# Squares of adj turned in place through three places, most mask pieces made by GpSimd, and a transposed copy with longer runs, in a four-layer graph network

## The chip, the cores and the metric

The kernel runs on one core of a Trainium2 chip. The metric is the time of one execution on the device in microseconds; less is better. The profile is one execution of the same program, taken by the hardware profiler. Its span is counted from the first to the last instruction, and the profiled execution's own time is a little more than its span. Engines are named as TensorE (PE), VectorE (DVE), ScalarE (ACT), GpSimd (POOL) and SyncE (SP), which here does nothing but issue DMAs and wait.

## The reference

There are 4096 nodes with 256 features in `x`, and a dense float32 `adj` of 4096 x 4096 in which about one entry in 130 isn't zero. Every layer is followed by a residual and a LayerNorm.

```python
def layer0(x, adj):                       # 4 heads of 64
    q, k, v = split(x @ Wqkv + bqkv)      # per head
    scores = q @ k.T * 64 ** -0.5 + graph_bias * adj
    scores = where(adj == 0, -1e9, scores)
    return softmax(scores) @ v @ Wout + bout
def layer1(x, adj):
    Wh = x @ W
    e = leaky_relu((Wh @ a[:256])[:, None] + (Wh @ a[256:])[None, :], 0.2)
    return softmax(where((adj > 0) | eye, e, -9e15), axis=1) @ Wh
def layer2(x, adj):                       # d = adj.sum(axis=1) ** -0.5
    return (d[:, None] * adj * d[None, :]) @ x @ W.T + b
def layer3(x, adj):
    return relu((d[:, None] * adj * d[None, :]) @ x @ W)
for layer in (layer0, layer1, layer2, layer3):
    x = layernorm(x + layer(x, adj))
```

## The kernel before, in words

The whole program is written by hand: every engine has its own list of instructions, in an order that the code fixes, and semaphores tie the lists together. There is no scheduler.

**Layer 0** (`layer0_attention`, to about 1740 us of the span) takes the 4096 rows in 16 chunks of 256. A chunk is a loop of 32 *beats*, numbered `at` = 8h + j for four heads h and eight pieces j of 128 x 1024 scores. In each beat TensorE makes one piece of scores (four matmuls, line 513) for the beat 12 later and VectorE reads it (line 757: it adds the bias, writes to a ring of probabilities and keeps the row maximum). TensorE has one PSUM place for such a piece, so the read must be over before TensorE's next scores. Besides, TensorE transposes earlier probabilities (line 525) in one beat and aggregates with the values (line 538) in odd beats, projects a finished head (line 547) at j = 3, and makes queries at the end of odd heads. ScalarE takes exponentials (643) and copies transposed probabilities out of PSUM (652).

The *bias* of a chunk (graph_bias * adj, plus a huge negative number where adj is zero) has eight pieces of 128 x 1024. While a chunk runs, the bias of the next is made in place: piece i is loaded by SyncE at beat 12 + i (`load_bias`, 341); VectorE makes a mask of it (`mask_bias`, 715: is_equal, to bf16) and then the bias (`make_bias`, 723). `BIAS_PARTS` says how many of these sixteen steps stand in which beat, 14 to 26. There is one buffer for masks. From beat 20 on, reads of scores use the new bias.

Layer 0 also writes `adjT`, a copy of adj in DRAM in which squares of 32 x 32 are transposed, for layers 2 and 3. It is made in 256 *blocks* of 128 x 512: SyncE loads a block (`load_block`, 352), VectorE turns it (`turn_block`, 777), SyncE stores it with four DMAs (`store_block`, 362). Before, a chunk has 16 blocks, in its odd beats; the last chunk has its 16 in two beats of three up to beat 23. A block is turned from one of two input buffers into one of two output buffers. SyncE stores block b in the beat after its turn, then loads block b + 2, and then, in even beats, waits until TensorE has aggregated in the next odd beat and reloads that quarter of the values (`load_values`, 337); next stand x and bias loads. All this is one queue, in this order. GpSimd has a power for each chunk's LayerNorm and the store of the chunk's rows.

The last chunk makes no bias. In its beats VectorE and SyncE do early work for layer 1 instead (`early_sync`: loads of x and of adj rows, of 2 MB each).

**Layer 1** (`graph_layers`, about 1740 to 2370 us) works on 8 chunks of 512 rows; masks of adj > 0 are made on VectorE and on GpSimd (line 1040), and `degrees` (1206) computes d, as 128 x 32 numbers, on GpSimd.

**Layers 2 and 3** (to the end) are 16 runs of 512 rows. Each run reads adjT in *sets* of 512 keys, four DMAs of 256 KB per set (`load_set`, 1126), with the four 32-row groups of a tile in separate pieces of 2 KB. The rows of x that meet them are loaded by `load_row_tile` (1142), scaled by d and split into a high and a low part (`split_hi`, 1454 on ScalarE, `split_lo` on VectorE). TensorE multiplies three times for each pair of tiles (1374 to 1376).

Of the kernel before, what the change touches and what calls it, by code (L numbers as in the profile page):

```python
# [23 lines left out]
P = 128  # L24
N = 4096
# [112 lines left out]
class Shared:  # L138


    def __init__(self, space, x1_stored):
# [3 lines left out]
        self.block_stored = [space.sem(f"block_stored{k}") for k in range(2)]  # L145
# [3 lines left out]
def layer0_attention(nc, shared, x, adj, Wqkv, bqkv, Wout, bout, graph_bias, v_heads, value_stored, x1, x1_stored, adjT):  # L149

# [23 lines left out]
    BIAS_PARTS = {14: 1, 15: 1, 16: 2, 17: 1, 18: 1, 19: 1, 20: 2, 21: 1, 22: 1, 23: 1, 24: 2, 25: 1, 26: 1}  # L174
# [14 lines left out]
    CHUNK_BLOCKS = CT * BLOCK_SETS  # L189
    BLOCKS = CHUNK_BLOCKS * CHUNKS  # L190
    SQUARE = 32
    SQUARES = P // SQUARE
    BLOCK_BEATS = tuple(range(1, CHUNK_BEATS, 2))
    LAST_BLOCK_BEATS = (1, 2, 4, 5, 7, 8, 10, 11, 13, 14, 16, 17, 19, 20, 22, 23)
    x_tiles, adj_tiles, x1_tiles, w_rows = tiles_of(x), tiles_of(adj), tiles_of(x1), tiles_of(Wqkv)
    with ExitStack() as ctx:
        sp = Space(nc, ctx, "at")
        kT = sp.sb("kT", [P, H, N], F32R)
        probs = sp.sb("probs", [P, 2 * CT * N])
        bias = sp.sb("bias", [P, CT, N])  # L200
        q = sp.sb("q", [P, 3, 2, CN], F32R)
        masked = sp.sb("masked", [P, PIECE], BF16)
# [19 lines left out]
        first = probs[:, 0:CT * N]  # L222
        ring = probs[:, 2 * CT * N - PLACES * CT * PIECE:].rearrange("p (k t n) -> p k t n", k=PLACES, t=CT)
        squares = probs[:, 0:4 * BLOCK].rearrange("p (a b n) -> p a b n", a=2, b=2)
# [15 lines left out]
        bk = first[:, 7680:7682]  # L240
# [20 lines left out]
        block_loaded = [sp.sem(f"block_loaded{k}") for k in range(2)]  # L261
        block_turned = sp.sem("block_turned")
        block_stored = shared.block_stored
        masked_ready = sp.sem("masked_ready")
# [19 lines left out]
        shared.blocks_stored = 16 * SQUARES * BLOCKS // 2  # L284
# [20 lines left out]
        def block_in(c, at):  # L305

            beats_of = LAST_BLOCK_BEATS if c == CHUNKS - 1 else BLOCK_BEATS
            return CHUNK_BLOCKS * c + beats_of.index(at) if at in beats_of else None

        def block_at(b):  # L310

            return b // CHUNK_BLOCKS * CT + b % CT, b % CHUNK_BLOCKS // CT

# [20 lines left out]
        def sync_program(sync, early):  # L334
# [15 lines left out]
            def load_block(b):  # L350
                row_tile, n = block_at(b)
                sync.dma_start(squares[:, 0, b % 2, :], adj_tiles[:, row_tile, n * BLOCK:(n + 1) * BLOCK])\
                    .then_inc(block_loaded[b % 2], 16)

            def store_block(b):
# [4 lines left out]
                for g in range(SQUARES):  # L360
                    at = row_tile % BLOCK_TILES * P + g * SQUARE
                    sync.dma_start(to[:, row_tile // BLOCK_TILES * BLOCK_SETS + n, :, at:at + SQUARE],  # L362
                                   squares[g * SQUARE:(g + 1) * SQUARE, 1, b % 2, :]
                                   .rearrange("j (k i) -> j k i", i=SQUARE))\
                        .then_inc(block_stored[b % 2], 16)
# [65 lines left out]
        def gpsimd_program(pool):  # L431
# [15 lines left out]
            for c in range(CHUNKS):  # L447
                finish(c)
# [1397 lines left out]
```

## Time and profile before

| what | before |
| --- | --- |
| time, median of 3 runs | 3175.77 us (3172.98 to 3178.01) |
| profiled execution, its own time | 3172.68 us |
| its span | 3170.9 us |
| TensorE busy | 3017.0 us, 95% |
| VectorE busy | 2140.6 us, 68% |
| ScalarE busy | 1893.5 us, 60% |
| GpSimd busy | 364.5 us, 11% |
| hardware DMA queue, share of 16 engines | 72.9% |
| granted clock of TensorE, mean | 0.99 |

A busy share is an average over four layers with different limits. What a change in one of them is worth is read from that stage: from the reads of scores for layer 0, since each stands for one beat, and from the chain of waits at the joints between layers.

### The profile page before, as it was taken

The numbers are of one execution on the slowest core, as the hardware profiler recorded it, in microseconds if no ns is written. First come the engines' busy times: TensorE is split into PE (matmuls) and PEld (weight loads), VectorE is DVE, ScalarE is ACT, GpSimd is POOL, SyncE is SP. The second block draws the span as 40 slices with busy tenths as digits, with TensorE's granted clock in tenths as the row PEclk, the third lists the DMA queues.
The fourth block names the chain that finished last, engine by engine and source line by source line (L and its number), as shares of the span: only waits on it lengthen the run. The fifth ranks groups of instructions, "written<-read, shape, count | busy, mean of one in ns | idle before, by whom it ended". The sixth has DMA issues, their size and how long they took to land.

```text
span 3170.9 us, 45180 instructions
## 1 busy us (share of the span) xinstructions
PE 3017.0 (95%) x16612; PEld 2174.3 (69%) x16612; DVE 2140.6 (68%) x3588; ACT 1893.5 (60%) x2705; POOL 364.5 (11%) x196
## 2 busy tenths in 40 slices
PE   8899999999999999999996899999999999799998
PEld 6676677766776677767774555555558888678886
DVE  6677776777677776777675787777635545464554
ACT  3677767676777677776764577776663333343342
POOL 2000000000000000000000355554500000000000
PEclk9999999999999999999998999999999999899999
DMA  6688888888888888888899433333169989699982
GB/s 184 129 166 175 182 170 158 171 180 180 157 168 176 181 176 155 172 178 182 164 158 241 154 113 146 127 143 129 47 163 220 210 201 205 158 207 209 205 196 58
DMA packets 768588, 530.48 MB, mean 167 GB/s; under 512 B 563568, under 2 KB 599408, under 8 KB 768368
## 3 DMA queue, kind: packets, MB, share of 16 engines
q1 hardware_dynamic: 762096, 506.61, 72.9%
q0 software_dynamic: 6272, 20.98, 2.0%
q8 instruction: 133, 2.18, 0.3%
q14 instruction: 87, 0.71, 0.1%
HBM read 439.36 MB, written 88.08 MB: 166 GB/s over the span
## 4 chain that ended last, share of the span: by engine, by line
PE 77%; DVE 8%; DMA 7%; issue 4%; SPq 2%; ACT 2%; DVEq 0%; POOL 0%; POOLq 0%; ACTq 0%
PE at_score L513 13%; PE gl_four L1324 12%; PE at_o L538 12%; PE at_turn L525 10%; PE gl_quad L1374 7%; PE gl_quad L1375 7%; PE gl_quad L1376 7%; PE gl_quad L1307 3%; DMA at_bias<-in_adj 3%; PE at_mixed L547 2%; DMA gl_early<-x 2%; DVE at_probs L757 2%; PE gl_four L1349 2%; DVE at_bias L723 2%; SPq L362 1%
## 5 line engine op out<-in xcount | busy, mean ns | idle before, releaser
L757 DVE CUSTOM_DVE_ANT_0 at_probs<-at_score,at_bias 128x1024 f32<-128x1024 f32 x509 | 621.1, 1220 | 338.5 <-PE at_score L513 335.8
L652 ACT ACTIVATE at_pT<-at_turn 128x1024 f32<-128x1024 f32 x512 | 521.2, 1019 | 333.7 <-PE at_turn L525 332.3
L513 PE MATMUL at_score<-at_kT,at_q 128*128 128x512 f32 x2036 | 610.8, 422 | 69.2 <-DVE at_maxima L757 68.8
L643 ACT ACTIVATE at_probs<-at_probs,at_minus_max 128x1024 f32<-128x1024 f32 x512 | 585.8, 1144 | 39.3 <-DVE at_minus_max L762 38.3
L538 PE MATMUL at_o<-at_pT,at_values 128*64 128x256 f32 x4096 | 502.0, 387 | 22.4 <-DMA at_values<-v_heads 22.4
L525 PE MATMUL at_turn<-all_ident,at_probs 128*128 128x128 f32 x4096 | 489.8, 273 | 0.0
L525 PEld LDWEIGHTS at_turn<-all_ident,at_probs 128*128 128x128 f32 x4096 | 463.4, 140 | 35.6 <-issue 1.7
L513 PEld LDWEIGHTS at_score<-at_kT,at_q 128*128 128x128 f32 x2036 | 350.7, 189 | 196.5 <-DVE at_maxima L757 127.7
L1324 PE MATMUL gl_four<-gl_early,gl_first_wh 128*128 128x512 f32 x1024 | 460.7, 593 | 1.9 <-ACT gl_early L1442 1.9
L1467 ACT ACTIVATE gl_split<-gl_units 128x1024 fp32r<-128x1024 f32 x256 | 263.6, 1055 | 276.8 <-PE gl_quad L1376 276.8
L538 PEld LDWEIGHTS at_o<-at_pT,at_values 128*64 128x64 f32 x4096 | 272.2, 137 | 227.7 <-issue 93.9
L1374 PE MATMUL gl_quad<-gl_split,gl_rows_hi 128*128 128x512 f32 x1024 | 406.1, 397 | 21.8 <-DVE gl_split L1655 21.8
L1375 PE MATMUL gl_quad<-gl_split,gl_rows_hi 128*128 128x512 f32 x1024 | 401.6, 392 | 0.0
L1376 PE MATMUL gl_quad<-gl_split,gl_rows_lo 128*128 128x512 f32 x1024 | 401.3, 392 | 0.0
L1655 DVE TENSOR_TENSOR gl_split<-gl_units,gl_split 128x1024 fp32r<-128x1024 f32 x256 | 306.1, 1221 | 115.9 <-ACT gl_split L1467 115.5
L1324 PEld LDWEIGHTS gl_four<-gl_early,gl_first_wh 128*128 128x128 f32 x1024 | 184.7, 190 | 186.4 <-issue 184.1
L1040 POOL TENSOR_SCALAR gl_first_weights<-gl_first_weights 128x1024 f32<-128x1024 f32 x57 | 238.3, 4181 | 275.3 <-ACT gl_first_weights L1424 275.3
L1374 PEld LDWEIGHTS gl_quad<-gl_split,gl_rows_hi 128*128 128x128 f32 x1024 | 194.2, 190 | 65.3 <-DVE gl_split L1655 24.9
L1442 ACT ACTIVATE gl_early<-gl_quad 128x1024 f32<-128x1024 f32 x128 | 130.9, 1022 | 159.6 <-PE gl_quad L1307 159.6
L1376 PEld LDWEIGHTS gl_quad<-gl_split,gl_rows_lo 128*128 128x128 f32 x1024 | 194.1, 190 | 40.9
L1375 PEld LDWEIGHTS gl_quad<-gl_split,gl_rows_hi 128*128 128x128 f32 x1024 | 194.3, 190 | 40.3 <-issue 0.2
L777 DVE STREAM_TRANSPOSE at_probs<-at_probs 128x512 f32<-128x512 f32 x256 | 180.9, 707 | 27.6 <-DMA at_probs<-in_adj 26.5
(121 smaller groups left out, 2650.4 us busy)
## 6 DMA issues: line engine op xcount, KB each, us to landing
gl_units<-adjT SPq DMA_DIRECT2D x512, 256.0 KB, 7.7
at_bias<-in_adj SPq DMA_DIRECT2D x128, 512.0 KB, 6.9
at_values<-v_heads SPq DMA_DIRECT2D x256, 256.0 KB, 4.0
at_probs<-in_adj SPq DMA_DIRECT2D x256, 256.0 KB, 5.0
adjT<-at_probs SPq DMA_DIRECT2D x1024, 64.0 KB, 4.0
gl_first_weights<-in_adj SPq DMA_DIRECT2D x32, 2048.0 KB, 8.1
gl_early<-x SPq DMA_DIRECT2D x24, 512.0 KB, 4.6
x<-gl_early POOLq DMA_DIRECT2D x16, 512.0 KB, 3.9
```

What stands on the lines that cost most here:

```text
L513: last = pe.matmul(place[:, at], q[:, q_place(h), part, t * P:(t + 1) * P], kT[:, h, col:col + BANK], start=part == 0, stop=part == 1)
L525: last = pe.transpose(turn_bank[j % 2][:, a * CN + t * P:a * CN + (t + 1) * P], ring[:, place_in_ring(s, m // BEATS), t, m % BEATS * P:(m ...
L538: last = pe.matmul(o_bank[side * HD:(side + 1) * HD, 0:CN], values[:, q, a, :], pT[:, slot, a % GROUP * CN:(a % GROUP + 1) * CN], start=q ...
L643: act.activation(part, part, ACT.Exp, bias=minus_max[:, k, t:t + 1], scale=1.0, accum_out=sums[:, k, t, pp:pp + 1]).then_inc(prob_ready, 1)
L652: act.activation(pT[:, j % PT_SLOTS, :], turn_bank[j % 2][:], ACT.Copy).then_inc(pT_ready, 1)
L757: dve.tensor_tensor_reduce(out=ring[:, place_in_ring(u, pp), t, :], in0=place[:], in1=bias[:, t, at], scale=SCALE, scalar=LOWEST, op0=ALU. ...
L1324: last = pe.matmul(out_bank1[c % 2][half], wh[:, m * D + half * P:m * D + (half + 1) * P], pT[:, g % PT_RING, part * CN:(part + 1) * CN], ...
L1374: pe.matmul(out_bank3[r % 2][half], rows_hi[:, at], block_hi, start=first, stop=False)
L1375: pe.matmul(out_bank3[r % 2][half], rows_hi[:, at], block_lo, start=False, stop=False)
L1376: last = pe.matmul(out_bank3[r % 2][half], rows_lo[:, at], block_hi, start=False, stop=final)
L1467: act.activation(split3[:, slot, 0, :], tiles[:, n, part:part + 2 * CN], ACT.Copy).then_inc(hi3_ready, 1)
L1655: dve.tensor_tensor(split3[:, slot, 1, :], tiles[:, n, part:part + 2 * CN], split3[:, slot, 0, :].bitcast(F32), ALU.subtract).then_inc(lo3 ...
```

## The change

Three things change in layer 0 and one in what layers 2 and 3 read.

1. The blocks are turned in place, in three buffers in place of two pairs. SyncE waits, before it loads block b + 2, until block b - 1 has been stored from the same place. The 256 blocks now stand in 17 beats of each chunk, `BLOCK_BEATS`, most of them even; 15 chunks take 255 blocks and the last chunk one.
2. Six of the eight mask pieces of a chunk's bias are made by GpSimd, as soon as the load has landed and the bias of two pieces before is made; there are two buffers for masks. VectorE makes the last two, in beats 24 and 25. The makes stand in beats 17, 18, 20, 21 and 23 to 26. On GpSimd the finish of a chunk now comes before the masks of the same turn of the loop.
3. The load of a set is one DMA of 1 MB with runs of four rows, 8 KB. The keys of a set so arrive in another order; `load_row_tile` loads the rows of x in the same order, and GpSimd makes a permuted copy of d in 32 small copies (`row_scale`), for which the first `split_hi` waits.
4. The views of a few layer 0 buffers move, and `masked` gets two places.

```diff
-        self.block_stored = [space.sem(f"block_stored{k}") for k in range(2)]
+        self.block_stored = [space.sem(f"block_stored{k}") for k in range(3)]
...
-    BIAS_PARTS = {14: 1, 15: 1, 16: 2, 17: 1, 18: 1, 19: 1, 20: 2, 21: 1, 22: 1, 23: 1, 24: 2, 25: 1, 26: 1}
+    MAKE_BIAS = {17: 0, 18: 1, 20: 2, 21: 3, 23: 4, 24: 5, 25: 6, 26: 7}
+    MASK_BIAS = {24: 6, 25: 7}
+    POOL_MASKS = 6
...
-    BLOCK_BEATS = tuple(range(1, CHUNK_BEATS, 2))
-    LAST_BLOCK_BEATS = (1, 2, 4, 5, 7, 8, 10, 11, 13, 14, 16, 17, 19, 20, 22, 23)
+    BLOCK_BEATS = (0, 2, 4, 6, 8, 10, 12, 13, 15, 18, 19, 21, 22, 26, 27, 29, 30)
...
-        probs = sp.sb("probs", [P, 2 * CT * N])
+        masked = sp.sb("masked", [P, 2, PIECE], BF16)
+        probs = sp.sb("probs", [P, BLOCK_PLACES * BLOCK + PLACES * CT * PIECE])
...
         def block_in(c, at):
 
-            beats_of = LAST_BLOCK_BEATS if c == CHUNKS - 1 else BLOCK_BEATS
-            return CHUNK_BLOCKS * c + beats_of.index(at) if at in beats_of else None
+            b = len(BLOCK_BEATS) * c + BLOCK_BEATS.index(at) if at in BLOCK_BEATS else BLOCKS
+            return b if b < BLOCKS else None
...
             def load_block(b):
                 row_tile, n = block_at(b)
-                sync.dma_start(squares[:, 0, b % 2, :], adj_tiles[:, row_tile, n * BLOCK:(n + 1) * BLOCK])\
-                    .then_inc(block_loaded[b % 2], 16)
+                sync.dma_start(squares[:, b % BLOCK_PLACES, :], adj_tiles[:, row_tile, n * BLOCK:(n + 1) * BLOCK])\
+                    .then_inc(block_loaded[b % BLOCK_PLACES], 16)
...
                         if b + 2 < BLOCKS:
+                            wait(sync, block_stored[(b + 2) % BLOCK_PLACES], 16 * SQUARES * ((b + 2) // BLOCK_PLACES))
                             load_block(b + 2)
...
+            def mask_bias(c, i):
+
+                t, pp = piece_at(i)
+                pool.wait_ge(adj_loaded[i], 16 * (c + 1))
+                pool.wait_ge(bias_ready, BEATS * c + i - 1)
+                pool.tensor_scalar(masked[:, i % 2, :], bias[:, t, pp * PIECE:(pp + 1) * PIECE], 0.0, MASKED / SCALE,
+                                   ALU.is_equal, ALU.mult).then_inc(masked_by_pool, 1)
+
             for c in range(CHUNKS):
-                finish(c)
+                if c:
+                    finish(c - 1)
+                if c + 1 < CHUNKS:
+                    for i in range(POOL_MASKS):
+                        mask_bias(c + 1, i)
+            finish(CHUNKS - 1)
...
             def turn_block(b):
 
-                dve.wait_ge(block_loaded[b % 2], 16 * (b // 2 + 1))
-                wait(dve, block_stored[b % 2], 16 * SQUARES * (b // 2))
-                dve.transpose(squares[:, 1, b % 2, :], squares[:, 0, b % 2, :]).then_inc(block_turned, 1)
+                dve.wait_ge(block_loaded[b % BLOCK_PLACES], 16 * (b // BLOCK_PLACES + 1))
+                part = squares[:, b % BLOCK_PLACES, :]
+                dve.transpose(part, part).then_inc(block_turned, 1)
...
-                for q in range(SQUARES):
-                    sync.dma_start(tiles[q * SQUARE:(q + 1) * SQUARE, n, :].rearrange("j (k r) -> j k r", k=KEPT),
-                                   kept[q, :, SETS * (r % CHUNKS) + n, :, :]).then_inc(tiles_loaded[n], 16)
+                kept = adjT.rearrange("j (g q x) -> q j g x", q=SQUARES, x=KEPT * CN)
+                sync.dma_start(tiles[:, n, :], kept[:, :, SETS * (r % CHUNKS) + n, :]).then_inc(tiles_loaded[n], 16)
...
-                sync.dma_start(xs[:, k % XS_RING, :], old_tiles[layer][:, m, :]).then_inc(xs_loaded[k % XS_RING], 16)
+                rows = old_rows[layer].rearrange("(s q k j) d -> s k q j d", q=SQUARES, k=KEPT, j=SQUARE)[m // KEPT, m % KEPT]
+                sync.dma_start(xs[:, k % XS_RING, :], rows).then_inc(xs_loaded[k % XS_RING], 16)
...
+                for scale, inv in zip(row_scale, inv_deg):
+                    for q in range(SQUARES):
+                        for k in range(KEPT):
+                            pool.tensor_copy(scale[q * SQUARE:(q + 1) * SQUARE, :].rearrange("p (s k) -> p s k", k=KEPT)[:, :, k],
+                                             inv[k * SQUARE:(k + 1) * SQUARE, :].rearrange("p (s q) -> p s q", q=SQUARES)[:, :, q])\
+                                .then_inc(degree_steps, 1)
...
                 if k == 0:
-                    act.wait_ge(degree_steps, 4)
+                    act.wait_ge(degree_steps, 4 + 2 * SQUARES * KEPT)
```

## Rows read from the trace of the kernel before

**Rows 1.** The page, parts 1 and 4: busy time by engine; chain of waits.

```profile
PE 3017.0 (95%) x16612; PEld 2174.3 (69%) x16612; DVE 2140.6 (68%) x3588; ACT 1893.5 (60%) x2705; POOL 364.5 (11%) x196
...
PE 77%; DVE 8%; DMA 7%; issue 4%; SPq 2%; ACT 2%; DVEq 0%; POOL 0%; POOLq 0%; ACTq 0%
```

**Rows 2.** Timeline, VectorE: start, duration, engine, line, out<-in, count, idle before and its releaser.

```profile
532.05 1.22 DVE L757 CUSTOM_DVE_ANT_0 at_probs<-at_score,at_bias 128x1024 f32<-128x1024 f32 x1 [1.33 <-PE at_score L513]
...
535.16 1.22 DVE L757 CUSTOM_DVE_ANT_0 at_probs<-at_score,at_bias 128x1024 f32<-128x1024 f32 x1 [0.59 <-PE at_score L513]
...
537.72 1.22 DVE L757 CUSTOM_DVE_ANT_0 at_probs<-at_score,at_bias 128x1024 f32<-128x1024 f32 x1 [1.14 <-PE at_score L513]
...
541.72 1.23 DVE L757 CUSTOM_DVE_ANT_0 at_probs<-at_score,at_bias 128x1024 f32<-128x1024 f32 x1 [1.63 <-PE at_score L513]
```

**Rows 3.** Timeline, VectorE: the block turned in beat 1 of chunks 1 and 15.

```profile
205.25 0.71 DVE L777 STREAM_TRANSPOSE at_probs<-at_probs 128x512 f32<-128x512 f32 x1
...
1629.26 0.71 DVE L777 STREAM_TRANSPOSE at_probs<-at_probs 128x512 f32<-128x512 f32 x1
```

**Rows 4.** Timeline, VectorE: the first mask of a chunk's bias, beat 14.

```profile
552.75 0.69 DVE L715 TENSOR_SCALAR at_masked<-at_bias 128x1024 bf16<-128x1024 f32 x1 [3.77 <-DMA at_bias<-in_adj]
```

**Rows 5.** Groups by line: count; busy us, mean ns of one; idle before, releaser.

```profile
L1040 POOL TENSOR_SCALAR gl_first_weights<-gl_first_weights 128x1024 f32<-128x1024 f32 x57 | 238.3, 4181 | 275.3 <-ACT gl_first_weights L1424 275.3
L777 DVE STREAM_TRANSPOSE at_probs<-at_probs 128x512 f32<-128x512 f32 x256 | 180.9, 707 | 27.6 <-DMA at_probs<-in_adj 26.5
L723 DVE SCALAR_TENSOR_TENSOR at_bias<-at_bias,at_gain,at_masked 128x1024 f32<-128x1024 f32 x128 | 163.8, 1280 | 1.3
L715 DVE TENSOR_SCALAR at_masked<-at_bias 128x1024 bf16<-128x1024 f32 x128 | 88.5, 691 | 58.0 <-DMA at_bias<-in_adj 55.5
...
L740 DVE SCALAR_TENSOR_TENSOR at_q<-at_mixed,at_bq,at_q 64x256 fp32r<-64x256 f32 x64 | 30.8, 481 | 1.1
```

**Rows 6.** Timeline, GpSimd and VectorE: masks of layer 1 on GpSimd beside VectorE.

```profile
2021.64 3.63 POOL L1040 TENSOR_SCALAR gl_first_weights<-gl_first_weights 128x1024 f32<-128x1024 f32 x1 [5.79 <-ACT gl_first_weights L1424]
2021.69 2.07 DVE L1561 CUSTOM_DVE_ANT_0 gl_first_weights<-gl_first_dst_row,gl_first_weights 128x1024 f32<-128x1024 f32 x1
...
2030.64 3.63 POOL L1040 TENSOR_SCALAR gl_first_weights<-gl_first_weights 128x1024 f32<-128x1024 f32 x1 [5.37 <-ACT gl_first_weights L1424]
2030.70 0.48 DVE L1626 SCALAR_TENSOR_TENSOR gl_early<-gl_four,gl_inv_sum,gl_early 128x256 f32<-128x256 f32 x1
```

**Rows 7.** Timeline, VectorE and SyncE: last chunk, from a block to the next but one.

```profile
1631.43 0.71 DVE L777 STREAM_TRANSPOSE at_probs<-at_probs 128x512 f32<-128x512 f32 x1
...
1634.90 2.94 SPq L362 DMA_DIRECT2D adjT<-at_probs  x4
...
1643.63 0.71 DVE L777 STREAM_TRANSPOSE at_probs<-at_probs 128x512 f32<-128x512 f32 x1 [1.97 <-DMA at_probs<-in_adj]
```

**Rows 8.** Timeline, SyncE and VectorE: stores and load of blocks beside bias loads.

```profile
572.01 4.51 SPq L362 DMA_DIRECT2D adjT<-at_probs  x4
576.56 2.55 SPq L352 DMA_DIRECT2D at_probs<-in_adj  x1
...
583.17 0.71 DVE L777 STREAM_TRANSPOSE at_probs<-at_probs 128x512 f32<-128x512 f32 x1 [0.73 <-DMA at_probs<-in_adj]
```

**Rows 9.** Timeline, SyncE and TensorE: the end of layer 0.

```profile
1707.59 13.21 SPq L362 DMA_DIRECT2D adjT<-at_probs  x4
...
1735.48 3.68 PE L538 MATMUL at_o<-at_pT,at_values 128*64 128x256 f32 x16 [15.51 <-DMA at_values<-v_heads]
```

**Rows 10.** Timeline, SyncE and ScalarE: the entry of layer 3.

```profile
2717.91 1.75 SPq L1126 DMA_DIRECT2D gl_units<-adjT  x4
...
2726.13 0.91 ACT L1454 ACTIVATE gl_rows_hi<-gl_early,gl_inv_deg 128x256 fp32r<-128x256 f32 x2 [7.76 <-DMA gl_early<-x]
...
2729.26 1.74 SPq L1126 DMA_DIRECT2D gl_units<-adjT  x4
```

**Rows 11.** Groups by line, GpSimd: an operation of 128x32.

```profile
L1212 POOL TENSOR_TENSOR gl_inv_deg<-gl_inv_deg,gl_no_row 128x32 f32<-128x32 f32 x1 | 0.3, 253 | 0.1
```

More of the change, by code:

```diff
@@ L239, in layer0_attention @@
         bv = in_first(7168, 2, D)
-        bk = first[:, 7680:7682]
+        bk = sp.sb("bk", [P, H // 2])
         v_out = pT[:, 0:2, :].rearrange("p k (t d) -> p k t d", t=RUN_TILES)
@@ L283, in layer0_attention @@
         shared.turned_but_one = BEATS * (UNITS - 1)
-        shared.blocks_stored = 16 * SQUARES * BLOCKS // 2
+        shared.blocks_stored = [16 * SQUARES * len(range(k, BLOCKS, BLOCK_PLACES)) for k in range(BLOCK_PLACES)]
         WEIGHT_LOADS = 2
@@ L713, in mask_bias @@
                 dve.wait_ge(adj_loaded[i], 16 * (c + 1))
[L714 to L715 removed]
+                wait(dve, bias_ready, BEATS * c + i - 1)
+                dve.tensor_scalar(masked[:, i % 2, :], bias[:, t, pp * PIECE:(pp + 1) * PIECE], 0.0, MASKED / SCALE,
                                   ALU.is_equal, ALU.mult).then_inc(masked_ready, 1)
@@ L721, in make_bias @@
                 part = bias[:, t, pp * PIECE:(pp + 1) * PIECE]
-                dve.wait_ge(masked_ready, BEATS * c + i + 1)
-                dve.scalar_tensor_tensor(out=part, in0=part, scalar=gain[:, 0:1], in1=masked[:],
+                if c and i < POOL_MASKS:
+                    dve.wait_ge(masked_by_pool, POOL_MASKS * (c - 1) + i + 1)
+                else:
+                    dve.wait_ge(masked_ready, (BEATS - POOL_MASKS) * c + i + 1)
+                dve.scalar_tensor_tensor(out=part, in0=part, scalar=gain[:, 0:1], in1=masked[:, i % 2, :],
                                          op0=ALU.mult, op1=ALU.add).then_inc(bias_ready, 1)
@@ L840, in body @@
                         ln.normalise(dve, acc, c - 1)
-                    for n in range(BIAS_PARTS.get(at, 0)):
-                        if not last:
-                            part = sum(many for when, many in BIAS_PARTS.items() if when < at) + n
-                            step = make_bias if part % 2 else mask_bias
-                            step(c + 1, part // 2)
+                    if at in MASK_BIAS and not last:
+                        mask_bias(c + 1, MASK_BIAS[at])
+                    if at in MAKE_BIAS and not last:
+                        make_bias(c + 1, MAKE_BIAS[at])
                     b = block_in(c, at)
@@ L1102, in early_sync @@
                 load_first_adj(sync, 3)
-                for stored in shared.block_stored:
-                    sync.wait_ge(stored, shared.blocks_stored)
+                for stored, blocks in zip(shared.block_stored, shared.blocks_stored):
+                    sync.wait_ge(stored, blocks)
                 load_second_adj(sync, 0)
```

39 lines of the change are left out of this document (19 added, 20 removed).

## The prediction, made before the changed kernel ran

> **What bounds the kernel now.** I read the page first: TensorE is busy for 3017.0 of 3170.9 us [rows 1], so only its gaps can be shortened, and an edit on another engine is worth what it closes or opens there. The chain of waits is next: TensorE has 77% of it, VectorE 8, DMAs 7, issue 4 [rows 1]. Read in order of time it stays on TensorE in the smooth part of each layer 0 chunk and leaves it in three places: where the next chunk's bias is made (beats 14 to 26), at the end of layer 0, and at the entry of layer 3.
>
> The timeline of VectorE gives the beat. The reads of scores start at 532.05, 535.16, 537.72 and 541.72: 3.11 us after an odd beat's, 2.56 after an even one's, 5.67 for a pair; with a projection the odd one has 4.00 [rows 2]. A read lasts 1.22, so VectorE has 1.34 us for other work in an even beat and 1.89 in an odd one (2.78 with a projection or query matmuls) without delaying anything. There is one score place, so TensorE waits if a read is late. A delay made in an even beat is forgiven up to 0.55 in the next, since the odd beat has that much air.
>
> A chunk is (1629.26 - 205.25) / 14 = 101.7 us [rows 3]. Without stalls: 16 x 5.67 = 90.7, four projections 4 x 0.89 = 3.6, two query matmul groups and the turn of x (an estimate of 2.2 from the projection's price) = 96.5. So 5.2 us of every chunk are stalls, 78 us over the 15 chunks that make a bias. One is the mask at beat 14, which waits 3.77 us for its load with the next read queued behind it [rows 4]; the others are beats with more VectorE work than room.
>
> **Masks and their timetable.** Six masks of 0.69 us leave VectorE per chunk; eight bias makes of 1.28 stay [rows 5]. By the windows above the new table costs: beats 16/17, odd 0.97 (query finish, two operations of 0.48) + 1.28 = 2.25 against 1.89: 0.4 [rows 5]. Beats 18/19: even 1.28 + 0.71 and 0.2 for the small one of the maxima = 2.2, a delay of 0.86 that the projection's air takes: 0. Beats 20/21: even 1.28 and the add step, at two operations of the same kind again 0.87 without their overlap, gives a delay of 0.8, odd 1.28 + 0.71 = 1.99: 0.8 + 1.99 - 1.89 = 0.9. Beats 24/25: 1.97 and 1.97: 0.63 + 1.97 - 1.89 = 0.7. Others fit; a square in beats 0, 4 and 12 gives delays under 0.4. Sum 2.0, so 98.5 us per chunk if nothing is late: -3.2 x 15 = -48 us.
>
> That holds if GpSimd is in time. Its mask in layer 1 took 3.63 us alone [rows 6] and 4.18 in the mean [rows 5], for another comparison and an f32 output; I take 4. With the read of beat 12 as zero, loads land at about 11, 15, 20, 20, 25, 25, so the six masks end at 15, 19, 24, 28, 32 and 36 (mask i+2 also waits for make i). The makes come at 17.5, 20, 27, 29, 35 and 39. The least margin is 1 us; if a mask took 5 us, two makes would be 1 us late (+15 us in all), if 3.6 nothing changes. On GpSimd nothing else waits there: the LayerNorm power and the x1 store of a chunk come before beat 14.
>
> GpSimd and VectorE meet at SBUF. A two-input VectorE operation that started 0.05 us after a GpSimd mask took 2.07 us instead of 1.22, ended inside the mask, and cost it nothing; one that reads PSUM and SBUF, as the read of scores does, kept its length beside a mask [rows 6]. So a make can lose 0.85 when it meets a mask's start, and makes mostly precede the mask that they release: 0 to 0.85 x 6 per chunk, I take 0.
>
> The Trainium skill (SBUF — State Buffer, Who interferes with whom) says more: the shared port pair is held "for the whole instruction" and the other side fully blocks. By that rule each make issued during a mask would wait for its end. The 0.85 us speak against it. It is a rival below.
>
> **The squares.** This part decides, I think. The transposition keeps its 0.71 us; in place or not costs nothing that rows show. What moves is where it stands against SyncE's queue. A block's path is: turned, four stores issued, load of the block after next issued, landed. SyncE handles a block in the beat after its turn, but in an even beat it first waits for the next beat's aggregation to reload values. A block turned in an odd beat is stored at once; one turned in an even beat stands behind that wait. The last chunk shows it: turned at 1631.43, stores from 1634.90 for 2.94 us, landed 1643.63, 11.5 us after the turn's end, and VectorE waited 1.97 [rows 7]. In the bias stretch a store group took 4.51, and a load issued at 576.56 landed at 583.17, 6.6 us later [rows 8].
>
> Today only odd beats are used, four beats from a block to the one that depends on it (11.3 us and more). The new table uses even beats mostly and leaves three beats in 10-13, 12-15, 18-21, 19-22, 26-29, 27-30 and 29-0.
> - Beat 15: turn 12 ends at 2.8, values 4.4, one bias load, stores from 5.2 to 8.3 or 9.7, landing 14 to 16.3; wanted at 10.0. 4 to 6.3 late, of which 2.06 fit the window: 2 to 4.3. I take 2.5.
> - Beat 21: turn 18 ends 3.4 after its read, values and bias issued by 5.2, stores to 9.2, landing 14.4 to 15.8; wanted at 11.5: 3 to 4.3, all of it felt on top of the 0.9. I take 3.5.
> - Beat 22: its load stands behind that one, a bias load and four more stores: 1 to 5 late, felt 0.5 to 3.9. I take 2.
> - Beats 8, 13, 29, 30, 0: 11.5 from turn to landing against 9 to 12 of distance: 0 to 2.5. I take 1.3.
> The added wait for the store of block b-1 (three places) lies behind four store issues of 2 us and more, so it adds under 1 us, inside these bounds; behind it stand the block load, values and bias loads.
> Sum 9.3 (5.5 to 15; 0 if loads land sooner than these rows): 98.5 + 9.3 = 107.8 us per chunk, +6.1 x 15 = +91 us.
>
> **The end of layer 0.** The last chunk had 16 blocks, now one. VectorE waited 26.5 us for block loads in the whole kernel [rows 5], nearly all there; its first 20 beats lose about 5 us: -5. After them SyncE is stuck in store groups, one of 13.21 us, and TensorE waits 15.51 us for values [rows 9]. The wait goes, but the 2 MB loads of layer 1 fill the queue by themselves, and VectorE still sums twelve pieces. Between -10 and -25; I take -18.
>
> **Layers 2 and 3.** TensorE is full in the steady part, so one 1 MB load in place of four of 256 KB gives nothing there, and permuted rows carry the same sums. At the entry of layer 3 SyncE alternates four set loads (1.75 us), four row tiles, and a ScalarE wait of 7.76 for these [rows 10]: rounds of 11.3 us (2717.91 to 2729.26), six of them. Three issues less save 1.3 a round, and the row tiles stand behind a transfer with 8 KB runs instead of 2 KB, at a guess 1.2 sooner: 6 x 2.5 = -15 (0 to -20). The 32 small GpSimd copies ahead of the first scaled row cost at most the 0.25 us of a 128x32 operation each [rows 11], 8 us, of which TensorE's copies ahead hide three: 0 to +5, I take +1.
>
> **Sum** against the profiled execution, 3172.7 us (1.8 outside its span): +91 - 5 - 18 - 15 + 1 = +54, 3227; the shown median stands 3.1 higher, and I forecast 3228 us.
>
> **Rivals.**
> 1. Loads in time: the even-beat delay is hidden, because a landing after 8 us of a turn suffices everywhere, and the masks' gain stays. For it: of 26.5 us of waits for block loads in the kernel the steady chunks of today have hardly any [rows 5]. Against: the 11.5 and 6.6 us of [rows 7, 8]. Time: -48 - 37 = -85, 3091. It decides when the waits of VectorE for block loads stay under 2 us per chunk.
> 2. A draw: about 5.7 us per chunk felt, the low end of my bounds. +2.5 x 15 = +37 against -37: 3176.
> 3. Late loads at the upper ends, since every lateness makes the queue later still: 15 felt, +11.8 x 15 = +177, with -37: near 3310.
> 4. The whole-instruction lock: four of six makes meet a running mask and wait for half of it, 1.8 us: 7.3 a chunk, half reaching TensorE, +55 on my forecast: 3283. For it only the rule, against it the 0.85 us.
>
> **Chances.** Forecast 0.52, rival 1 0.27, rival 2 0.08, rival 3 0.09, rival 4 0.04. The forecast's own range is 3185 to 3275; with the others 8 in 10 lie between 3085 and 3290. No change means within 0.2%, 6 us, about what this kernel's measurement tells: faster 0.29, same 0.08, slower 0.63.
>
> **What would show it.** Right: VectorE waits for block loads of some 10 us per chunk, at beats 15, 21 and 22; chunks near 107 us; no mask wait; in the last chunk almost none of either; row tile rounds under 10 us. Wrong: chunks near 98 us and no such waits (rival 1), or makes of 2 us and more beside masks (rival 4), or makes that wait for masks (GpSimd slower than 5 us).

## The result and the profile after

The changed kernel takes 3879.36 us (median of 4 runs, 3876.08 to 3885.07) against 3176.89 before (four runs; the table above has the first three): a ratio of 1.2217, 95% interval 1.2202 to 1.2231. Forecast were 3228, and no case of the prediction reached 3400. The page of the changed kernel (busy time; granted clock, DMA share and rate in 40 slices; first queue; chain of waits), to be held against [rows 1]:

```profile
PE 3213.6 (83%) x16612; PEld 2281.0 (59%) x16612; DVE 2084.8 (54%) x3498; ACT 1892.6 (49%) x2705; POOL 689.0 (18%) x318
...
PEclk9999999999999999999999998988888667988888
DMA  5788888888889888866233321223222222322222
GB/s 167 153 178 167 158 158 165 166 171 171 170 166 176 172 167 156 160 137 228 108 130 127 145 98 58 114 113 116 112 113 118 107 66 98 116 113 116 113 113 90
...
q1 hardware_dynamic: 704496, 506.58, 51.6%
...
PE 40%; DMA 36%; SPq 11%; DVE 8%; issue 3%; ACT 2%; POOL 1%; DVEq 0%; POOLq 0%; ACTq 0%
```

The chain was 77% TensorE, now it is 40%, and the DMAs' part went from 7 to 36. The last 16 slices tell where: 113 GB/s at a busy share of two to three tenths, with everything waiting for it. Engines that wait for DMAs while the DMA engines stand idle for seven tenths are the picture to remember. Waits of the changed kernel (us in total, times, longest):

```profile
ACT gl_split L1493 <- DMA gl_units<-adjT: 751.4, 92, 10.2
...
POOL at_masked L455 <- DMA at_bias<-in_adj: 451.9, 45, 56.8
...
DVE at_probs L796 <- DMA at_probs<-in_adj: 258.3, 108, 4.7
```

By the start of the last aggregation of layer 0, and of the first product of layer 2, the span divides so:

| stretch | before | after | difference |
| --- | --- | --- | --- |
| layer 0, to its last aggregation | 1738.5 | 1803.2 | +64.7 |
| layer 1, to the first product of layer 2 | 633.6 | 667.1 | +33.5 |
| layers 2 and 3 | 798.8 | 1408.7 | +609.9 |
| span | 3170.9 | 3879.0 | +708.1 |

Layers 2 and 3 in the steady part, first before, then after (columns: PE, PEld, DVE, ACT, POOL busy, granted clock, DMA share, GB/s):

```profile
2372.00:2700.00 328.00, 328.00 (x1455) 272.48 (x1454) 178.45 (x248) 120.02 (x124) 19.02 (x14) 1.00 0.95 209
```

```profile
2480.00:3200.00 720.00, 430.85 (x1552) 336.64 (x1550) 199.12 (x287) 129.72 (x146) 15.69 (x15) 0.78 0.28 107
```

And SyncE there: the issue of a set of 1 MB takes it 9.5 us in the median, where each quarter of a set took 0.43 before (timeline of the changed kernel; [rows 10] had four issues in 1.75):

```profile
3026.34 9.77 SPq L1154 DMA_DIRECT2D gl_early<-x  x1
3036.15 30.64 SPq L1145 DMA_DIRECT2D gl_units<-adjT  x4
```

At 107 GB/s a set of 1 MB takes 9.8 us. The share, 0.28, is near 4 of 16 engines.

Layer 0 is another matter. Its chunks, read as in [rows 3] from the block of beat 0, last (1710.44 - 207.68) / 14 = 107.3 us; the prediction had 107.8.

```profile
207.68 0.71 DVE L796 STREAM_TRANSPOSE at_probs<-at_probs 128x512 f32<-128x512 f32 x1
...
1710.44 0.71 DVE L796 STREAM_TRANSPOSE at_probs<-at_probs 128x512 f32<-128x512 f32 x1
```

VectorE's waits for blocks stand in the beats that it named: per chunk 3.3 us in beat 15, 3.7 in 21, 3.5 in 22, some 4 in 13, 29 and 30 together, and, which it did not name, 2.5 in beat 19. Beats 21 and 22 of one chunk, on VectorE:

```profile
707.79 0.71 DVE L796 STREAM_TRANSPOSE at_probs<-at_probs 128x512 f32<-128x512 f32 x1 [4.25 <-DMA at_probs<-in_adj]
712.78 0.71 DVE L796 STREAM_TRANSPOSE at_probs<-at_probs 128x512 f32<-128x512 f32 x1 [3.16 <-DMA at_probs<-in_adj]
```

### The profile page after: what moved, and what is told of

Its sections match the earlier page's. It is cut to its first block, busy times and chain, and to the rows that moved or that the text cites. A ratio compares the mean times of both kernels' runs of the same rounds, so it can differ in the third digit from the quotient of the medians.

```text
span 3879.0 us, 44573 instructions
## 1 busy us (share of the span) xinstructions
PE 3213.6 (83%) x16612; PEld 2281.0 (59%) x16612; DVE 2084.8 (54%) x3498; ACT 1892.6 (49%) x2705; POOL 689.0 (18%) x318
## 4 chain that ended last, share of the span: by engine, by line
PE 40%; DMA 36%; SPq 11%; DVE 8%; issue 3%; ACT 2%; POOL 1%; DVEq 0%; POOLq 0%; ACTq 0%
DMA gl_units<-adjT 24%; PE at_score L529 9%; PE gl_four L1350 9%; PE at_o L554 8%; PE at_turn L541 7%; DMA gl_early<-x 6%; DMA at_probs<-in_adj 4%; SPq L364 4%; DVE at_probs L776 3%; PE gl_quad L1333 2%; SPq L1145 2%; SPq L1161 2%; DVE at_bias L742 1%; PE at_mixed L563 1%; DVE gl_split L1681 1%
## 5 line engine op out<-in xcount | busy, mean ns | idle before, releaser
L1400 PE MATMUL gl_quad<-gl_split,gl_rows_hi 128*128 128x512 f32 x1024 | 470.7, 460 | 475.5 <-DVE gl_split L1681 475.3
L529 PE MATMUL at_score<-at_kT,at_q 128*128 128x512 f32 x2036 | 623.3, 429 | 112.3 <-DVE at_maxima L776 111.2
L1400 PEld LDWEIGHTS gl_quad<-gl_split,gl_rows_hi 128*128 128x128 f32 x1024 | 225.7, 220 | 563.4 <-DVE gl_split L1681 514.3
L554 PE MATMUL at_o<-at_pT,at_values 128*64 128x256 f32 x4096 | 522.7, 399 | 10.0 <-DMA at_values<-v_heads 9.9
L1350 PE MATMUL gl_four<-gl_early,gl_first_wh 128*128 128x512 f32 x1024 | 464.1, 596 | 26.8 <-ACT gl_early L1468 26.8
L1401 PE MATMUL gl_quad<-gl_split,gl_rows_hi 128*128 128x512 f32 x1024 | 452.3, 442 | 0.0
L1402 PE MATMUL gl_quad<-gl_split,gl_rows_lo 128*128 128x512 f32 x1024 | 450.0, 439 | 0.0
L554 PEld LDWEIGHTS at_o<-at_pT,at_values 128*64 128x64 f32 x4096 | 281.0, 142 | 228.1 <-issue 112.7
L455 POOL TENSOR_SCALAR at_masked<-at_bias 128x1024 bf16<-128x1024 f32 x90 | 327.0, 3645 | 477.3 <-DMA at_bias<-in_adj 451.9
L796 DVE STREAM_TRANSPOSE at_probs<-at_probs 128x512 f32<-128x512 f32 x256 | 181.0, 707 | 259.2 <-DMA at_probs<-in_adj 258.3
L128 POOL TENSOR_TENSOR gl_ln_rstd<-gl_ln_var_eps,gl_ln_minus_half 128x4 f32<-128x4 f32 x24 | 29.1, 1214 | 1296.6 <-DVE gl_ln_var_eps L120 1296.3
L1402 PEld LDWEIGHTS gl_quad<-gl_split,gl_rows_lo 128*128 128x128 f32 x1024 | 224.2, 219 | 54.1
```

Source lines behind the costliest of these rows:

```text
L455: pool.tensor_scalar(masked[:, i % 2, :], bias[:, t, pp * PIECE:(pp + 1) * PIECE], 0.0, MASKED / SCALE, ALU.is_equal, ALU.mult).then_inc(m ...
L529: last = pe.matmul(place[:, at], q[:, q_place(h), part, t * P:(t + 1) * P], kT[:, h, col:col + BANK], start=part == 0, stop=part == 1)
L554: last = pe.matmul(o_bank[side * HD:(side + 1) * HD, 0:CN], values[:, q, a, :], pT[:, slot, a % GROUP * CN:(a % GROUP + 1) * CN], start=q ...
L1350: last = pe.matmul(out_bank1[c % 2][half], wh[:, m * D + half * P:m * D + (half + 1) * P], pT[:, g % PT_RING, part * CN:(part + 1) * CN], ...
L1400: pe.matmul(out_bank3[r % 2][half], rows_hi[:, at], block_hi, start=first, stop=False)
L1401: pe.matmul(out_bank3[r % 2][half], rows_hi[:, at], block_lo, start=False, stop=False)
```

## The experiments

Unless said otherwise a time is a median of four runs or more, and the ratio is to the kernel before on the same chip. Medians of the kernel before differ by up to 6.5 us between chips, so runs of two groups are compared by their ratios. "Chunk" is the mean of chunks 1 to 14, from the reads of scores at beat 0.

### The sets of layers 2 and 3

**Sets by 32 rows.**

```diff
-                sync.dma_start(tiles[:, n, :], kept[:, :, SETS * (r % CHUNKS) + n, :]).then_inc(tiles_loaded[n], 16)
+                for q in range(SQUARES):
+                    sync.dma_start(tiles[q * SQUARE:(q + 1) * SQUARE, n, :], kept[q, :, SETS * (r % CHUNKS) + n, :])\
+                        .then_inc(tiles_loaded[n], 16)
...
-                act.wait_ge(tiles_loaded[n], 16 * (r + 1))
+                act.wait_ge(tiles_loaded[n], 16 * SQUARES * (r + 1))
```

> The changed kernel with each set loaded by four DMAs of 32 partitions x 8 KB (outermost dimension 32) in place of one DMA whose outermost dimension is 4; same bytes, same 8 KB runs, same places; the row tiles keep their outermost dimension of 4. Theory A (a DMA with an outermost dimension of 4 runs on 4 of the 16 engines: in layers 2 and 3 the changed kernel moves 107 to 113 GB/s at a DMA busy share of 0.28): the loads run at over 200 GB/s again, layers 2 and 3 lose most of their 610 us, the row tiles still cost 20 to 50 us at the entries: 3260 to 3300 us. Theory B (8 KB runs of adjT are slow to read): nothing changes, about 3880. Theory C (one DMA per set leaves too little in flight): as A here.

3272.06 us, ratio 1.0285 (1.0266 to 1.0304), as theory A had it. Layers 2 and 3 take 807.4 us. The same bytes in the same 8 KB runs now move at 209 GB/s, with TensorE full:

```profile
2461.00:2790.00 329.00, 329.00 (x1459) 273.13 (x1458) 179.02 (x248) 120.99 (x124) 19.00 (x14) 1.00 0.92 209
```

So the 8 KB runs are not slow (theory B falls); they are not faster than the 2 KB runs before either, 209 GB/s both, at a share of 0.92 against 0.95.

**Sets by 64 rows**: the same loop over `q in (0, 2)`, each DMA taking `kept[q:q + 2]`, so that the outermost dimension is 2.

> The changed kernel with each set loaded by two DMAs of 64 partitions, outermost dimension 2. Theory A: two engines of sixteen, the same two for both: each set takes twice as long, some 19 us in place of 9.8, 128 x 9.5 = 1200 us more: about 5100 us. Theory B: no change, 3880. Theory C (too few DMAs in flight): two in flight help: below 3880.

5150.5 us (one run). Twice as many DMAs, half the rate, half the share (window of this kernel, columns as above):

```profile
2600.00:3900.00 1300.00, 448.86 (x1455) 346.53 (x1456) 189.82 (x270) 127.28 (x144) 12.86 (x14) 0.65 0.15 57
```

Rate and share follow the outermost dimension: 32 gives 209 GB/s at 0.92 (there TensorE is the limit), 4 gives 107 at 0.28, 2 gives 57 at 0.15. That is 26.8 and 28.5 GB/s for each of 4 and 2 engines, if these are the engines that work; the trace gives only the mean share of all 16. Theory C falls with it.

The Trainium skill has this rule (DMA: Bandwidth & Descriptors, "Why a DMA increments its semaphore by 16 and not by 1"): a DMA is spread over the largest number of engines up to 16 that divides the slowest dimension of both its sides, and its rules for kernel authors say to put a multiple of 16 outermost. By that rule the trace agrees in all three cases. The change's destination, all 128 partitions, looks as if it met it; the source, `q j x` with q = 4, does not.

**Sets and row tiles by 32 rows**: the row tiles of x, whose source has the same outermost 4, are loaded by four DMAs too.

> As the one before, and each row tile of x loaded by four DMAs of 32 partitions too. Theory A: layers 1 to 3 at the pace of the kernel before or a little better, and only layer 0's loss stays (last aggregation 64.7 us later): 3225 to 3242 us. If the permuted rows or the 32 small copies cost by themselves, it stays above 3260.

3277.43 us, 1.0295 (1.0276 to 1.0315): theory A missed, and the time is that of the run before within the noise. Layer 0 keeps its loss, but layer 1 takes 655.9 us (652.6 in the run before) where the kernel before took 633.6. Row tiles loaded by four times the DMAs gain nothing; whether the issues eat up what more engines give was not taken apart.

**The layer 2 and 3 part alone**, on the kernel before.

> The kernel before with the layer 2 and 3 part of the change alone (one DMA per set, permuted row tiles, 32 copies on GpSimd); layer 0 as before. Theory A: 3176.9 + 610 for layers 2 and 3 + 33 at the end of layer 1 = about 3820 us, the last aggregation of layer 0 where it was (1738 us). If layer 0's new timetable is part of the loss of the later layers, clearly less than 3820.

3819.57 us, 1.2000 (1.1980 to 1.2021), as expected: layers 2 and 3 take 1408.7 us, exactly those of the changed kernel, and layer 1 31.7 more than before. The two parts of the change hardly touch each other.

**What layer 1 still loses.** Of the run by 32 rows, once the 32 copies are left out (scales read from `inv_deg`), once the row tiles come in natural order by one DMA of 128 partitions. Both kernels leave out the matching of rows, scales and keys, so layers 2 and 3 compute other numbers with the same work:

> The changed kernel with sets by 32 rows and without the 32 small copies on GpSimd: the scales are read where they were made (so layers 2 and 3 compute with other numbers). The copies took 7.96 us of GpSimd ahead of the first scaled row. Theory H (the copies are what layer 1 lost beyond the sets, 19 us in the run by 32 rows): 3250 to 3260 us, layer 1 near 640. Theory I (the permuted row tiles are): within 4 us of that run's 3272.

> The changed kernel with sets by 32 rows and the row tiles of x loaded in their natural order by one DMA of 128 partitions each (so rows meet the wrong keys: other numbers); the copies stay. Theory I (row tiles whose outermost dimension is 4 arrive late): layer 1 10 to 15 us shorter and the entry of layer 3 too, 3250 to 3260 us. Theory H: within 4 us of 3272.

3253.79 us (1.0253, 1.0237 to 1.0270) and 3248.12 us (1.0236, 1.0221 to 1.0251). Layer 1's turns (first to last start of its transposes) take 561.7 us before, 579.5 in the run by 32 rows, 571.1 without the copies, 568.4 with the tiles in order. Both are part of it. By the ratios, the copies cost 10 us and the permuted tiles 16; layer 1 is 8.1 and 10.9 us shorter without them (652.6 against 644.5 and 641.7), and the tiles in order also take 5.8 us off layers 2 and 3. The copies are GpSimd's last work ahead of the first scaled row, for which ScalarE waits 6.8 us; after it ScalarE, in order, waits for late row tiles while TensorE waits for it. GpSimd's two new operations in the changed kernel (groups by line):

```profile
L455 POOL TENSOR_SCALAR at_masked<-at_bias 128x1024 bf16<-128x1024 f32 x90 | 327.0, 3645 | 477.3 <-DMA at_bias<-in_adj 451.9 <-DVE at_bias L742 25.4
L1236 POOL COPY gl_row_scale<-gl_inv_deg 32x8 f32<-32x8 f32 x32 | 6.2, 193 | 1.9
```

ScalarE's waits for row tiles, with the tiles permuted and then in order:

```profile
ACT gl_rows_hi L1482 <- DMA gl_early<-x: 108.9, 42, 11.4
```

```profile
ACT gl_rows_hi L1481 <- DMA gl_early<-x: 75.1, 11, 10.5
```

### Layer 0

**The layer 0 part alone** (layers 2 and 3 as before):

> The layer 0 part of the change alone; sets, row tiles and scales of layers 2 and 3 as in the kernel before. The chunks of the changed kernel take 107.3 us against 101.7 and its last aggregation ends 64.7 us later, so: 3181 + 65 = 3246 us (3236 to 3256), with chunks of 107 us.

3241.96 us, 1.0205 (1.0189 to 1.0220), chunk 107.3, as expected. This is the change without the sets. The forecast without its two terms for the later layers is 3228 + 15 - 1 = 3242.

**The load of block b + 2 ahead of the stores of b**: `store_block(b)` moves below `load_block(b + 2)` and its wait.

> The layer 0 part alone, with one order turned on SyncE: the load of block b + 2 is issued ahead of the four stores of block b (its place was freed by the stores of b - 1). Theory D (the loss is late block loads: 258.3 us of VectorE waits in 15 chunks): loads land 2 to 4.5 us sooner, most of the waits go, chunks of 100 to 103 us: 3150 to 3190 us. Theory G (GpSimd's masks beside VectorE cost it, or even beats have too little room): under 15 us gained, over 3225.

3318.35 us, 1.0443 (1.0428 to 1.0459), chunk 113.1: both theories missed. SyncE now stands in its wait until the stores just issued have landed, with the next stores behind it (timeline of this kernel):

```profile
458.87 0.35 SPq L354 DMA_DIRECT2D at_probs<-in_adj  x1
459.27 2.14 SPq L364 DMA_DIRECT2D adjT<-at_probs  x4
461.45 0.52 SPq L339 DMA_DIRECT2D at_values<-v_heads  x1
465.35 0.35 SPq L354 DMA_DIRECT2D at_probs<-in_adj  x1
```

The cycle of a block is 6.2 us (452.55 to 477.38 in four), longer than the 5.67 of a pair of beats. In the change's own order four issues cover that wait.

**Four places, with that order**, masks on VectorE with one buffer in place of two, to make room.

> As the run that loads ahead of the stores, but with a fourth place, so that load b + 2 waits for the stores of b - 2, long landed; all masks on VectorE in the old beats with one buffer, to make room. To be read against the run with masks on VectorE (chunks of 107.5, 3242 us). If the loss of the load-ahead run (113.1) came from its wait for the stores just issued, it goes: chunks of 107 or less. If late loads come from the stores ahead of them in the queue, chunks of 103 to 105 and 3180 to 3205 us; if from full DMA engines, 106 to 108 and 3220 to 3250.

3204.56 us, 1.0096 (1.0077 to 1.0114), chunk 105.0. This is, just, what was expected if the stores ahead of the loads in the queue make them late. Against 107.5 of the next run it gains 2.5; VectorE's waits for blocks all but vanish (132.3 to 11.0 us) with the stores as they were, but those for bias loads rise from 66.6 to 93.2, in which the single mask buffer may have a part. The order decides whose load is late; 3.3 us of the chunk's loss against the kernel before stay.

**All masks on VectorE again**, blocks in the new beats:

> The layer 0 part alone, with all masks on VectorE again in the beats of the kernel before (two mask buffers stay), blocks in the new beats. Theory D: the masks come back on top of late loads; some of their time hides in the waits: chunks of 108 to 111 us, 3255 to 3300 us. Theory G: contention goes, chunks of 104 to 106: below 3230.

3242.28 us, 1.0217 (1.0195 to 1.0240), chunk 107.5: the same time as with GpSimd's masks. Neither theory had that. Six masks of 0.69 us [rows 5], 4.1 us of VectorE's work per chunk, are worth nothing here: VectorE waits 132.3 us for blocks in place of 251.6, so what the masks take the waits give back.

**Blocks in the odd beats of before**, GpSimd's masks kept; and with **masks on VectorE too**:

> The layer 0 part alone, with the blocks in the beats of the kernel before (16 odd ones, and 16 in the last chunk); three places, turned in place, six masks by GpSimd. Theory D: waits for block loads nearly gone, the masks' gain shows, though odd beats 17, 21, 23 and 25 carry a make and a block: chunks of 99 to 101 us, the end of layer 0 as before: 3140 to 3175 us. Theory G: chunks stay above 104 us, over 3215.

> The run with blocks in odd beats, with all masks on VectorE in the beats of before as well: of the layer 0 part only the turning in place in three places is left. Theory P (three places and the added wait for stores cost nothing by themselves): as the kernel before, 3170 to 3182 us, chunks of 101.7, so that GpSimd's masks are what costs the other run its 1.8 us per chunk. Theory Q (they cost): chunks of 103 us or more, over 3190.

3196.14 us (1.0056, 1.0039 to 1.0072), chunk 103.5, and 3183.01 us (1.0023, 1.0012 to 1.0034), chunk 102.3. For the first, both theories missed; the second lies between its two, nearer to P. The new beats cost 3.8 of the 5.6 us per chunk with GpSimd's masks, and 5.2 with VectorE's (107.5 against 102.3). Three places in place cost little: 0.2%. And with GpSimd's masks the kernel is slower than without. What they save at beat 14 (2.9 us) comes back at beats 21 and 23, where blocks are late. The window of beats 16 to 27 in the odd-beat run with GpSimd's masks:

```profile
661.20:702.60 41.40, 37.08 (x251) 26.82 (x250) 32.97 (x55) 27.64 (x40) 20.09 (x6) 1.00 0.98 192
```

The DMA engines are full. Theory D2, formed here: the stores of squares, in runs of 128 B, fill the sixteen engines beside the bias loads. (In the kernel before the same beats show 0.96, with its chunk of 101.7, so a full share alone is not a loss.)

**Long store runs**: the same bytes by the same number of DMAs in runs of 2 KB. These three kernels leave out the order of elements that layers 2 and 3 need, so those compute other numbers with the same work.

```diff
-                    sync.dma_start(to[:, row_tile // BLOCK_TILES * BLOCK_SETS + n, :, at:at + SQUARE],
+                    sync.dma_start(to[:, row_tile // BLOCK_TILES * BLOCK_SETS + n, at // SQUARE, :],
...
-                                   .rearrange("j (k i) -> j k i", i=SQUARE))\
+                                   )\
```

> The run with blocks in odd beats and six masks by GpSimd, with each store of squares writing the same 64 KB in runs of 2 KB in place of 128 B (adjT then holds its elements in another order, so layers 2 and 3 compute with other numbers). Theory D2 (the 16 DMA engines are full beside the bias: busy share 0.94 to 1.12 in beats 16 to 27): block loads land in time, beats 21, 23 and 25 shrink, chunks of 99 to 100.5 us: 3130 to 3155. Theory G (GpSimd's masks take VectorE's time): chunks stay at 103: over 3185.

> The kernel before with the same long store runs. Theory D2: the bias loads land sooner and the stall at beat 14 (3.77 us for its mask) shrinks: chunks of 99.5 to 101 us, 3140 to 3170. If the stall hangs on the order of the queue alone: chunks of 101.7 and no change.

> The layer 0 part of the change as it is (17 blocks in its own, mostly even beats, six masks by GpSimd) with store runs of 2 KB in place of 128 B (adjT's elements in another order, other numbers in layers 2 and 3). Theory D1, as the prediction had it (a block turned in an even beat stands behind the wait for the values in SyncE's queue, whatever the stores weigh): waits of VectorE for block loads stay at several us per chunk, chunks over 102 us, over 3160. Theory D2 (the stores' packets fill the DMA engines): waits gone, chunks of 98.5 to 100, and with the 20 us of the end 3085 to 3115 us.

| with runs of 2 KB | us | ratio, interval | chunk, with 128 B |
| --- | --- | --- | --- |
| odd beats, GpSimd's masks | 3117.01 | 0.9816 (0.9801 to 0.9831) | 98.8, 103.5 |
| kernel before | 3158.43 | 0.9945 (0.9930 to 0.9960) | 101.6, 101.7 |
| the change's beats and masks | 3111.08 | 0.9794 (0.9776 to 0.9813) | 98.9, 107.3 |

The same twelve beats of the last of these (columns as above):

```profile
639.90:678.10 38.20, 36.75 (x250) 26.75 (x249) 32.84 (x54) 27.63 (x40) 19.26 (x6) 1.00 0.67 215
```

More bytes per us at two thirds of the engines' time. The long runs give the change's layer 0 8.4 us per chunk, and it is then worth what it was meant for: 2.7 against the kernel before with the same stores. D1 fails, though VectorE still waits 62.7 us in all for blocks (258.3 with 128 B), part of it within the air of the beats. That the kernel before keeps its chunks is a miss of D2: beat 14 takes 5.6 us in it with either stores. It gains at the end of layer 0 (from the read at beat 0 of the last chunk 99.6 us against 114.1).

What D2 leaves open is where the long runs help, since they relieve SyncE too. Stores of the block of beat 18 of chunk 5 and the load behind them, in the changed kernel and then with runs of 2 KB (timelines, SyncE):

```profile
697.13 4.21 SPq L364 DMA_DIRECT2D adjT<-at_probs  x4
701.38 2.35 SPq L354 DMA_DIRECT2D at_probs<-in_adj  x1
```

```profile
651.34 1.83 SPq L364 DMA_DIRECT2D adjT<-at_probs  x4
653.21 0.44 SPq L354 DMA_DIRECT2D at_probs<-in_adj  x1
```

In the mean of chunks 1 to 14 a block's turn and the landing of the load that follows it lie 10.3 us apart with runs of 128 B and 8.2 with 2 KB: 2.5 and 2.1 until the stores are issued, 2.6 and 2.1 for issuing them, 1.4 and 0.4 for issuing the load, the same DMA in both, and 3.7 and 3.5 from there to its landing. So nearly all of the gain stands in SyncE's queue. In beats 16 to 27 of the odd-beat run SyncE issues for 89% of the time, and for 52% with the long runs. Whether full engines hold the issues back, or short-run stores are slow to issue by themselves, isn't separated; the same stores issued by another engine would tell, and that wasn't tried.

**Runs of 256 B, same result**: the kernel before with blocks of two row tiles x 256 keys, VectorE turning into another order of squares, rows put back where layers 2 and 3 leave PSUM; and the same with 17 blocks per chunk. The same 17 beats with 128 B, three places and VectorE's masks came first.

```diff
...
-                dve.transpose(squares[:, 1, b % 2, :], squares[:, 0, b % 2, :]).then_inc(block_turned, 1)
+                dve.transpose(squares[:, 1, b % 2, :].rearrange("p (k t i) -> p k t i", t=2, i=SQUARE),
+                              squares[:, 0, b % 2, :].rearrange("p (t k i) -> p k t i", t=2, i=SQUARE)).then_inc(block_turned, 1)
...
-            copy(outT[:, half, :], bank).then_inc(outT_ready[half], 1)
+                copy(outT[:, half, :].rearrange("p (u g i) -> p u g i", g=SQUARES, i=SQUARE),
+                     bank.rearrange("p (g u i) -> p u g i", u=CT, i=SQUARE)).then_inc(outT_ready[half], 1)
```

> Masks on VectorE as before, three places, 17 blocks per chunk in beats 0, 2, 4, 6, 8, 10, 11, 13, 15, 17, 19, 21, 23, 25, 27, 28, 30: even ones only where the change of beats cost nothing (beats 0 to 11 took 35.8 us in both kernels), odd ones beside the bias. By that, chunks of 101.7 to 103 us, and the last chunk and its end 19 us shorter, as in the changed kernel: 3155 to 3180 us. If even beats cost wherever they are: over 3200.

> The kernel before with blocks of two row tiles x 256 keys, turned into an order in which stores have runs of 256 B in place of 128, and the rows put in order again where layers 2 and 3 leave PSUM: half the packets of the stores, same result. With 2 KB runs the kernel before gained 18 us, all of it in the last chunk and its end; with half the packets I expect half of it: 3163 to 3172 us. If the wider strides of VectorE's turn cost it: over 3180.

> As w1 with 17 blocks per chunk in beats 0, 2, 4, 6, 8, 10, 11, 13, 15, 17, 19, 21, 23, 25, 27, 28, 30 and one in the last chunk. With stores of 128 B these beats cost 2.9 us a chunk and the end gave 19 back; if the cost was the full DMA engines, half the packets take half of it or more away: chunks of 101.7 to 103, 3145 to 3165 us. If it was the order of the queue: chunks near 104.6, over 3180.

3194.87 us (1.0057, 1.0040 to 1.0074; chunk 104.6, a miss), 3160.53 us (0.9958, 0.9945 to 0.9971; chunk 101.4) and 3164.86 us (0.9967, 0.9954 to 0.9980; chunk 102.1). The second is 0.4% faster than the kernel before and so beats both kernels; with 17 blocks it is no faster. In beats 16 to 27 it differs from the kernel before by the share, 0.76 against 0.96, and hardly in time (its window, then that of before); its gain is at the end of layer 0, 101.0 us against 114.1.

```profile
654.40:693.40 39.00, 36.48 (x248) 26.43 (x247) 34.90 (x60) 26.51 (x40) 0.00 (x0) 1.00 0.76 201
```

```profile
658.10:697.20 39.10, 36.57 (x247) 26.39 (x246) 34.86 (x59) 26.28 (x38) 0.00 (x0) 1.00 0.96 202
```

GpSimd's masks on top of it, the mix that the 2 KB runs speak for, weren't tried.

## Why the prediction was wrong

**The step that failed** is in "Layers 2 and 3": "one 1 MB load in place of four of 256 KB gives nothing there". It counted issues and bytes, and asked whether TensorE would notice a faster load; it never asked on how many engines the new load runs. It runs on four, and the term "-15 (0 to -20)" measured +610, and layer 1 lost 33 more. The same part put a permuted row tile at a gain; it is a loss. Its "+1" for the copies measured about 8 us of layer 1 (652.6 against 644.5; 10 by the ratios): ScalarE stood still for 6.8 us until they were made.

**No rival and no bound held it.** The kernel before has single DMAs of 2 MB (32 of them, 8.1 us from issue to landing), but none whose source is led by a dimension of 4, so the new load should have been bounded from both sides like the other unknown costs. The prediction named a rule of the Trainium skill on ports that did not matter, and passed over the one on a DMA's outermost dimension, cited above, that did.

**The forecast of layer 0** was 107.8 us per chunk, measured 107.3. It adds 98.5 without late loads and 9.3 for these; the chunk with loads nearly in time, that with 2 KB runs, is 98.9, and 8.4 come on top. Late block loads in beats 15, 21 and 22 were named, and SyncE's queue was the place to look: with the load moved ahead the waits for blocks all but vanish. But the order was half of it. With the packets kept and the order improved the chunk falls only from 107.5 to 105.0, as other loads are late instead; with the order kept and the packets gone it falls from 107.3 to 98.9. The prediction took the time of an issue from rows and had no term for what makes it long. VectorE waited 17.2 us per chunk for blocks where "some 10" stood. For the end, "-5 - 18" measured -19.2 (from the read at beat 0 of the last chunk to the last aggregation 94.9 us against 114.1); TensorE's wait for the values, which was to go, is still 9.86 us in place of 15.51 [rows 9]. The last sum has a slip of its own: 3227 and 3.1 are 3230, not 3228.

**The masks**: "-3.2" per chunk measured 2.8 where the DMA engines have room (101.6 against 98.8) and nothing where they have not (107.3 against 107.5). That "-3.2" and "9.3" add up to the measured chunk is in part luck, since they don't add in the runs: with VectorE's masks the chunk is the same. A stall removed beside a full resource returns a few beats later. GpSimd took 3.65 us a mask where I took 4, and no make waited for one.

**Rival 4** (the whole-instruction lock) is out: 27 of the 128 bias makes began inside a running mask of GpSimd, and 25 of them kept their 1.28 us; the other two took 1.64 and 2.06, and VectorE never waited for a mask. The section of the Trainium skill that the prediction quotes (SBUF — State Buffer, Who interferes with whom) says "for the whole instruction" of VectorE's 2-port modes, and of an operation with two SBUF inputs, as a make is, only that it contends. Rival 1 was wrong in this kernel, but it is what the change's layer 0 does once stores are cheap.

## What to carry to other kernels

Before a DMA's shape is changed, read the outermost dimension of both sides: here it went with how many of the 16 engines worked. The sign in the profile was an engine waiting for a DMA while the DMA share was low. Where the share is near 1, or the issuing engine's queue has no gaps, count packets and issue time, not bytes, before work is taken off an engine beside it: here the time came back as another wait.

## What the runs showed of the hardware

- A DMA whose source had the outermost dimension 4 or 2 moved 107 or 57 GB/s, and SyncE's own issue of it then took 9.5 us in the median of either, in place of 0.43 for a quarter of a set with the outermost dimension 32.
- Half the packets for the stores' 64 MB (256 B in place of 128 B) took the queue's share over the span from 72.9% to 64.1%, 2 KB runs to 59.1%. The median block load, counted from the start of its issue, fell from 5.0 us to 3.6 and 3.3, and its issue alone from 1.0 to 0.5 and 0.4. All this is of the kernel before and its two variants.
  The Trainium skill (DMA: Bandwidth & Descriptors, Specifications) asks for transfers of 512 B or more for line rate; the three lengths here agree with it in their direction, and 512 B itself was not run.
- The stalls also cost clock. In beats 20 to 23 of one chunk TensorE was granted 0.82, between its levels of 1.2 and 2.4 GHz, after waits of VectorE for blocks, with TensorE busy for 14.2 of 18.7 us; in layers 2 and 3 it was 0.78 while TensorE was busy for 431 of 720 us. The aggregation's matmuls took 399 ns in the mean against 387.
- VectorE's transposition kept its 0.71 us in place, and with squares written in another order.
